# Gated experts and second MLP on one core: eight row slots, x of tiles 7 to 18 turned by VectorE, and loads issued by ScalarE

## Chip, cores and metric
One core of one Trainium2 chip runs the kernel. The metric is the device time of one execution in microseconds, the median of several runs. Engines: TensorE (PE), VectorE (DVE), ScalarE (ACT), GpSimd (POOL), SyncE (SP).

## What is computed
```python
# x: 2048 rows of 512; four experts, a token's id picks one
def experts(h, ids, W):                      # W[e]: 512 x 512, used three times
    e = min(clip(ids, 0, 24999) // 6250, 3)
    return (silu(h @ W[e].T) * (h @ W[e].T)) @ W[e].T
def mlp(h):                                  # 512 -> 1408 -> 512
    g = (h @ gate_w.T) * gate_s
    u = (h @ up_w.T) * up_s
    return (silu(g) * u) @ down_w.T * down_s
x = x + tanh(g_xattn) * experts(layernorm(x), ids, ctx)
x = x + tanh(g_ffn) * mlp(layernorm(x))
```
All three matrices of an expert are the same ctx_2048[e], so the kernel makes one product where gate and up have the same matrix. Each operand is split in a high part and the remainder, and a product runs in three passes (high x high, low x high, high x low).

## The kernel before, in words
**Routing.** A short part at the start sorts the tokens by expert into tiles of 128 rows of one expert each, at most 19 (`STEPS`), and makes the tables of row numbers `gidx` (gather) and `sidx` (store).

**Expert part.** Step k on PE: `first_product(k)` (12 matmuls; inner state z), `turn_x(k+1)` while x is turned by PE, `second_product(k-1)` (12 matmuls, waits `rows_ready` k, so for `update(k-2)`), and `turn_h(k)` (4 transposes of the hidden tile, waits `h_ready`). A tile goes this way: POOL gathers its rows into slot `ring_slot(k)` of `rows` (`gather`, L404), DVE makes its statistics (`stats`, L758), POOL the inverse deviation (`inverse_std`, L427), DVE the normalised tile (`norm`, L773, into `xn`), then x is turned (rows to columns), ACT writes the high part (`x_hi` or `turned_hi`), DVE the low part (`x_lo` or `turned_lo`). After the products DVE adds the result to the rows in the slot (`update`, L829), and POOL stores them to DRAM (`store`, L410). The slot is free when the store has landed: the gather of tile k+4 waits for store k-2, by one counter for all stores (L473).

**Two ways to turn x.** For tiles below `ON_PE` (11) PE turns it. From tile 11 on, SP's queue writes `xn` to DRAM and reads it back quarter by quarter (`turn_rows`, L336 to L345: first leg `turned_rows<-xn`, second leg `xq<-turned_rows`), and DVE transposes the 32x32 blocks of it (`turn`, L837, line L842). `norm(n+11)` waits until the first leg before it has landed; the second leg waits until the `turn` before it is done. Below it is called a bounce; bounce n is that of tile n + `ON_PE`.

**DVE's order in a step** is written out by hand: `step_on_pe(k)` (L851) is h_lo(k-1), norm(k+1), stats(k+2), hidden(k), x_lo(k+1), update(k-1); `step(k)` (L873), from k = 10 on, is h_lo(k-1), norm(k+2), turn(k+1-11), hidden(k), first half of the statistics of tile k+3, turned_lo(k+1), second half of them, update(k-1). hidden(k) (L820, "product" below) multiplies silu(z) by z and sets `h_ready`. `last_on_pe(9)` lies between. `first_stats(t)` (L787) makes the statistics of block row t of the second MLP's first block: 0 and 1 before step 9, 2 and 3 after steps 11 and 13.

**Loads.** Beside the bounces SP's queue holds, in written order, the MLP's weight rows (`weight_row`, L296, 704 KB each, eight), the down weights' check rows (`check_row`, L301, 256 KB each, eleven; each waits until ACT's `down_check` has freed its buffer) and the loads of the first block's rows (`load_half(0, 0)` and `(0, 1)`, L322, 528 KB each), which wait for the stores of their tokens. ACT in a step (L583): h_hi(k-1), weight_hi and weight_check of half a weight row, silu(k), x_hi or turned_hi of tile k+1, down_check.

**Second MLP.** Four blocks of four tiles, eleven chunks each: gate and up product (L1283), silu, product, down product (L1290). It starts when the last expert tile is in. Its first block's x comes from `first_norm`, `first_turn_x` (PE, L1147), `first_x_hi` and `first_x_lo` in steps 14 to 17, into the x buffer behind the expert weights in `work`, where `xq0`, `xt0` and `checked` lie before.

Of the kernel before, what the change touches and what calls it, by code (L numbers as in the profile page):

```python
# [39 lines left out]
RING = 6  # L40
ROWS = RING + BLOCK
# [6 lines left out]
PACKED = 15  # L48
EPS = 1e-5
# [5 lines left out]
ON_PE = 11  # L55
# [11 lines left out]
def ring_slot(k):  # L67

    return (k + 4) % RING


def row_slot(b, t):

    return t + RING * ((b + 1) % 2)
# [7 lines left out]
def build(nc, x, ids, ctxT, g_x, g_f, guT, dwT, gate_s, up_s, down_s, out):  # L82
# [7 lines left out]
    with ExitStack() as ctx:  # L90
# [12 lines left out]
        work = sb("work", [P, CTX_WORDS + XBUF_WORDS], F32R)  # L103
# [42 lines left out]
        xt0 = nc.alloc_sbuf_tensor_at("xt0", [P, D], F32, offset=work_base + (CTX_WORDS + 3 * D) * 4)  # L146
        wraw = nc.alloc_sbuf_tensor_at("wraw", [P, 2 * KC, 2, INTER], F32, offset=wgu_base)
# [65 lines left out]
        def token_of(first, last):  # L213

            return rows[:, first:last, D:D + 1].bitcast(U32)
# [30 lines left out]
        def quarter_rows(expert=False):  # L246

            return xq0[:, :] if expert else rows[:, RING - 2, 0:D]

        def turned_x(expert=False):  # L250

            return xt0[:, :] if expert else rows[:, RING - 1, 0:D]
# [4 lines left out]
        def down_w(c, s):  # L257
# [3 lines left out]
            row_landed w_hi w_lo down_hi down_lo  stored rows_a rows_b  # L261
# [9 lines left out]
        down_landed = [sem(f"down_landed{n}") for n in range(4)]  # L271
        last_stored = [sem(f"last_stored{t}") for t in range(BLOCK)]

        def hold(eng):

            eng.sem_inc(S["held"])

# [3 lines left out]
        def _(sp):  # L281
# [14 lines left out]
            def weight_row(r):  # L296
                if r:
                    sp.wait_ge(S["row_landed"], 16 * r)
                sp.dma_start(wraw[:, r, 1, :], gu_v[r // KC, r % KC]).then_inc(S["row_landed"], 16)

            def check_row(c):  # L301
                if c:
                    sp.wait_ge(S["check_landed"], 16 * c)
                if c >= 2:
                    sp.wait_ge(S["checks_done"], c)
                sp.dma_start(checked[:, c % 2, :], dw_v[c]).then_inc(S["check_landed"], 16)

            weight_row(0)
            check_row(0)
            check_row(1)  # L310
            weight_row(1)
            check_row(2)
            weight_row(2)
            check_row(3)
            sp.wait_ge(S["route_pe"], 4)
            sp.wait_ge(S["tables_ready"], 3)
            weight_row(3)
            check_row(4)
            weight_row(4)
            sp.wait_ge(S["ctx_lo"], len(ON_VECTOR))  # L320
            sp.wait_ge(S["pool_ctx_lo"], len(ON_POOL))
            def load_half(b, half_):  # L322
                t = BLOCK * b + 2 * half_
                at = row_slot(b, 2 * half_)
                if b == 0:
                    sp.wait_ge(S["stored"], 16 * (t + 2 + EXPERTS - 1))
                sp.dma_start(rows[:, at:at + 2, :], x1_v[:, t:t + 2, :])\
                  .then_inc((S["rows_a"], S["rows_b"])[half_], 16)

            for r in range(5, 2 * KC):  # L330
                check_row(r)
                weight_row(r)
            load_half(0, 0)
            check_row(8)

            def turn_rows(n):  # L336
# [3 lines left out]
                             xn[:, :].rearrange("p (i c) -> p i c", i=QUADS)).then_inc(S["xn_out"], 16)  # L340
# [6 lines left out]
            turn_rows(0)  # L347
            load_half(0, 1)
            check_row(9)
            turn_rows(1)  # L350
            check_row(10)
            for n in range(2, AHEAD):
                turn_rows(n)
            for c in range(IC):
                if c < 4:
                    sp.wait_ge(S["stored"], 16 * (TILES + c))
# [16 lines left out]
        def _(pool):  # L373
# [30 lines left out]
            def gather(k):  # L404
                at = ring_slot(k)
                pool.indirect_dma_start(  # L406
                    rows[:, at, 0:D], None, x, bass.IndirectOffsetOnAxis(ap=gidx[:, k:k + 1], axis=0))\
                    .then_inc(slot_landed[at], 16)

            def store(k):  # L410
                pool.indirect_dma_start(  # L411
                    scratch, bass.IndirectOffsetOnAxis(ap=sidx[:, k:k + 1], axis=0),
                    rows[:, ring_slot(k), :], None).then_inc(S["stored"], 16)
# [8 lines left out]
            def token_in(k, count=1):  # L422
                at = ring_slot(k)
                pool.tensor_copy(token_of(at, at + count), gidx[:, k:k + count].unsqueeze(2))\
# [7 lines left out]
            def first_inverse_std():  # L432
# [7 lines left out]
                rows[0:16, ring_slot(5), 0:D], None, x,  # L440
                bass.IndirectOffsetOnAxis(ap=inow[0:16, 0:1], axis=0)).then_inc(S["early_row"], 16)
            pool.memset(rows[:, 0:RING, D:WIDE], 0.0).then_inc(S["pads"], 1)
# [7 lines left out]
            pool.wait_ge(S["pads"], 1)  # L450
            token_in(0, 2)
            token_in(2, 4)
# [30 lines left out]
            for b in range(BLOCKS):  # L483
# [3 lines left out]
                for u in range(BLOCK):  # L487
# [6 lines left out]
                    else:  # L494
                        done = last_stored[t]
                    pool.indirect_dma_start(  # L496
                        out, bass.IndirectOffsetOnAxis(ap=token_of(row_slot(b, t), row_slot(b, t) + 1)[:, 0, :], axis=0),
# [3 lines left out]
        def _(act):  # L501
# [81 lines left out]
            def step(k, on_pe=False):  # L583
                h_hi(k - 1)
                weight_hi(k - PIECES_AT)
# [816 lines left out]
```

## Time and profile before
| | us |
|---|---|
| median of 3 runs | 386.21 |
| lowest, highest | 384.73, 387.35 |
| the profiled execution's own time | 384.71 |
| its span in the profile | 382.6 |
| PE busy | 364.2 (95% of the span) |
| DVE, ACT, POOL busy | 244.6, 147.5, 92.5 |

The span runs from the first to the last recorded instruction; 2.1 us of the execution's time lie around it. TensorE was granted its full clock nearly throughout. A step's bounds are taken at the start of `first_product` on PE; step 9 starts at 72.83 us, and the second MLP at 135.5 us.

### The profile page before, as it was taken

How to read it: one execution, taken by the hardware profiler on the slowest of the kernel's cores; microseconds unless marked ns; L12 is line 12 of the kernel's file. 1: busy time of each engine (PE TensorE's matmuls, PEld its weight loads, DVE VectorE, ACT ScalarE, POOL GpSimd, SP SyncE). 2: the span in 40 equal slices, each digit the busy share in tenths (PEclk: the TensorE clock that was granted, in tenths of full speed). 3: DMA queues.
4: the chain of work that ended last, by engine and by line, in shares of the span. 5: the costliest groups of instructions: out<-in, count | busy, mean ns of one | idle time of the engine just before them, and what ended most of it. 6: DMA issues, size and time to landing. Idle time of an engine off the chain costs nothing.

```text
span 382.6 us, 5569 instructions
## 1 busy us (share of the span) xinstructions
PE 364.2 (95%) x1704; PEld 298.0 (78%) x1704; DVE 244.6 (64%) x451; ACT 147.5 (39%) x266; POOL 92.5 (24%) x131
## 2 busy tenths in 40 slices
PE   3899999997999999999999999999999999999993
PEld 2478888786888878888888888888888888888892
DVE  6877666767998878779856256647346757323353
ACT  3466565646654536323322222322222322222230
POOL 7497454343461220011003110002201001300022
PEclk9999999999999999999999999999999999999998
DMA  6768876756654246432301412301232310200002
GB/s 224 274 217 259 260 275 195 261 142 222 218 165 142 84 140 192 140 86 57 82 0 55 169 55 83 82 0 55 76 119 69 95 27 27 82 0 0 0 29 86
DMA packets 27281, 45.39 MB, mean 119 GB/s; under 512 B 2928, under 2 KB 13168, under 8 KB 27264
## 3 DMA queue, kind: packets, MB, share of 16 engines
q1 hardware_dynamic: 22912, 30.83, 25.8%
q0 software_dynamic: 4352, 14.35, 10.4%
q8 instruction: 9, 0.15, 0.2%
q14 instruction: 8, 0.07, 0.1%
HBM read 30.59 MB, written 14.57 MB: 118 GB/s over the span
## 4 chain that ended last, share of the span: by engine, by line
PE 85%; DVE 6%; DMA 5%; issue 2%; POOL 1%; SPq 0%; ACT 0%; DVEq 0%; POOLq 0%
PE bank L1283 41%; PE bank L1178 21%; PE bank L1290 20%; DMA turned_rows<-xn 2%; PE bank L1193 2%; DMA rows<-x,gidx 2%; PE bank L1157 1%; DMA xq<-turned_rows 1%; PE bank L1147 0%; DVE rows L1060 0%; DMA ids_i<-ids 0%; DVE tmp L1053 0%; DVE parts L808 0%; DVE bn L763 0%; DVE xn L1053 0%
## 5 line engine op out<-in xcount | busy, mean ns | idle before, releaser
L1283 PE MATMUL bank<-work,wgu 128*128 (+1 forms) x736 | 167.3, 380 | 0.1
L1283 PEld LDWEIGHTS bank<-work,wgu 128*128 128x128 f32 x736 | 133.9, 188 | 27.1 <-issue 0.5
L1178 PE MATMUL bank<-work,parts 128*128 (+1 forms) x432 | 106.3, 397 | 2.0 <-ACT parts L522 1.7
L1178 PEld LDWEIGHTS bank<-work,parts 128*128 128x128 f32 x432 | 79.0, 188 | 18.8 <-issue 2.4
L1290 PE MATMUL bank<-work,hp 128*128 128x512 f32 x352 | 87.3, 390 | 0.2 <-DVE hp L1019 0.2
L1290 PEld LDWEIGHTS bank<-work,hp 128*128 128x128 f32 x352 | 65.7, 188 | 14.4 <-DVE hp L1019 0.6
L1000 DVE SCALAR_TENSOR_TENSOR sh<-bank,gs,sh 128x512 f32<-128x512 f32 x42 | 31.5, 749 | 55.4 <-PE bank L1283 55.4
L630 ACT ACTIVATE hp<-sh 128x512 fp32r<-128x512 f32 x42 | 26.6, 632 | 78.5 <-DVE sh L1000 78.5
L625 ACT ACTIVATE sh<-bank,gs 128x512 f32<-128x512 f32 x42 | 28.9, 688 | 72.0 <-PE bank L1283 71.2
L496 POOL DMA_INDIRECT out<-rows x16 | 16.2, 1011 | 128.3 <-DVE rows L1060 105.8
L1006 DVE TENSOR_TENSOR hp<-sh,hp 128x512 fp32r<-128x512 f32 x42 | 29.0, 691 | 22.3 <-ACT hp L630 22.3
L429 POOL TENSOR_TENSOR rstd<-ve,half 128x1 f32<-128x1 f32 x31 | 17.5, 564 | 104.4 <-DVE ve L770 104.2
L411 POOL DMA_INDIRECT x_rows<-rows,sidx x19 | 19.5, 1028 | 28.3 <-DVE rows L833 21.0
L406 POOL DMA_INDIRECT rows<-x,gidx x19 | 20.0, 1052 | 23.9 <-DMA x_rows<-rows,sidx 20.6
L763 DVE BATCH_NORM_STATS2 bn<-rows 128x6 f32<-128x512 f32 (+1 forms) x31 | 21.2, 684 | 0.8 <-DMA rows<-x,gidx 0.6
L531 ACT ACTIVATE parts<-bank 128x512 fp32r<-128x512 f32 x19 | 11.3, 596 | 25.0 <-PE bank L1193 22.5
L833 DVE SCALAR_TENSOR_TENSOR rows<-bank,tg,rows 128x512 f32<-128x512 f32 x19 | 14.2, 748 | 9.4 <-PE bank L1178 9.4
L822 DVE TENSOR_TENSOR sh<-bank,sh 128x512 f32<-128x512 f32 x19 | 13.1, 689 | 6.9 <-ACT sh L535 6.8
L535 ACT ACTIVATE sh<-bank 128x512 f32<-128x512 f32 x19 | 11.4, 598 | 12.5 <-PE bank L1178 11.1
L1043 DVE TENSOR_TENSOR work<-rows,work 128x512 f32 (+1 forms) x12 | 8.3, 692 | 9.7 <-ACT work L526 9.7
L826 DVE TENSOR_TENSOR parts<-bank,parts 128x512 fp32r<-128x512 f32 x19 | 13.0, 685 | 2.0 <-ACT parts L531 1.7
L842 DVE STREAM_TRANSPOSE rows<-rows 128x512 f32<-128x512 f32 x12 | 13.4, 1117 | 0.0
(134 smaller groups left out, 267.8 us busy)
## 6 DMA issues: line engine op xcount, KB each, us to landing
wraw<-guT SPq DMA_DIRECT2D x8, 704.0 KB
turned_rows<-xn SPq DMA_DIRECT2D x20, 256.0 KB
rows<-x_rows SPq DMA_DIRECT2D x8, 528.0 KB, 4.5
ctx_in<-ctxT SPq DMA_DIRECT2D x4, 1024.0 KB, 5.5
rows<-turned_rows SPq DMA_DIRECT2D x12, 256.0 KB
checked<-dwT SPq DMA_DIRECT2D x11, 256.0 KB
rows<-dwT SPq DMA_DIRECT2D x11, 256.0 KB, 2.8
xq<-turned_rows SPq DMA_DIRECT2D x8, 256.0 KB
```

The costliest lines, as they stand in the source:

```text
L406: pool.indirect_dma_start(rows[:, at, 0:D], None, x, bass.IndirectOffsetOnAxis(ap=gidx[:, k:k + 1], axis=0))\
L411: pool.indirect_dma_start(scratch, bass.IndirectOffsetOnAxis(ap=sidx[:, k:k + 1], axis=0), rows[:, ring_slot(k), :], None).then_inc(S["sto ...
L429: pool.tensor_tensor(rstd[:, 0:1], ve[:, 0:1], half[:, :], ALU.pow)\
L496: pool.indirect_dma_start(out, bass.IndirectOffsetOnAxis(ap=token_of(row_slot(b, t), row_slot(b, t) + 1)[:, 0, :], axis=0), rows[:, row_sl ...
L625: act.activation(sh[:, :], g_ps[:, :], ACT.Silu, scale=gs[:, 0, c:c + 1])\
L630: act.activation(hslot(c)[:, 0, :], sh[:, :], ACT.Copy).then_inc(S["hhi_ready"], 1)
L763: dve.bn_stats(bn[:, 0, :], rows[:, ds(at, 1), 0:D]).then_inc(S["bn_parts"], 1)
L1000: dve.scalar_tensor_tensor(out=sh[:, :], in0=u_ps[:, :], scalar=gs[:, 1, c:c + 1], in1=sh[:, :], op0=ALU.mult, op1=ALU.mult).then_inc(S["h ...
L1006: dve.tensor_tensor(hslot(c)[:, 1, :], sh[:, :], hslot(c)[:, 0, :].bitcast(F32), ALU.subtract).then_inc(S["hlo_ready"], 1)
L1178: mm = pe.matmul(out_ps[:, :], part(s)[:, c * P:(c + 1) * P], ctx_w(e, c, w), start=n == 0, stop=n == last)
L1283: mm = pe.matmul(out_ps[:, tiles.start * P:tiles.stop * P], wgu[:, row + h, w, c * P:(c + 1) * P], moving, start=n == 0, stop=n == last)
L1290: mm = pe.matmul(acc_ps[u][:, :], hslot(c)[:, s, u * P:(u + 1) * P], down_w(c, w), start=c == 0 and n == 0, stop=c == IC - 1 and n == len( ...
```

## The change
- `RING` goes from 6 to 8 row slots. Slots 6 and 7 (`far`) lie in the second MLP's x buffer in `work`; the MLP's own row slots stay where they were (`NEAR` = 6). Stores count on two semaphores, even and odd tiles (`tile_stored`). A gather is made for tile k+5 in POOL's iteration k and waits for store k-3.
- `ON_PE` goes from 11 to 7: x of tiles 7 to 18 is bounced and turned by DVE. The normalised tile for it has a buffer of its own (`xn_q`).
- DVE's `step(k)`, now from k = 6 on, makes turn, statistics of tile k+3, hidden, turned_lo, norm(k+3), then from k = 10 to 13 the statistics of block row k-10, and update last.
- Check rows 4 to 10 are issued by ACT in steps 5 to 11, weight rows 4 to 7 in steps 5, 7, 9 and 11 (`LOADS_AT`). ACT's loops over steps are written out. SP's queue holds the twelve bounces, `load_half(0, 0)` behind bounce 5 and `load_half(0, 1)` behind bounce 7.

```diff
-RING = 6
-ROWS = RING + BLOCK
+RING = 8
+NEAR = 6
+ROWS = NEAR + BLOCK
+LOADS_AT = {5: 4, 7: 5, 9: 6, 11: 7}
-ON_PE = 11
+ON_PE = 7
...
 def ring_slot(k):
-    return (k + 4) % RING
+    return (k + 2) % RING
...
+        xn_q = nc.alloc_sbuf_tensor_at("xn_q", [P, D], F32, offset=work_base + CTX_WORDS * 4)
+        far = nc.alloc_sbuf_tensor_at("far", [P, RING - NEAR, WIDE], F32,
+                                      offset=work_base + (CTX_WORDS + 6 * D) * 4)
+        def ring_rows(k, count=1):
+            at = ring_slot(k)
+            return rows[:, at:at + count, :] if at < NEAR else far[:, at - NEAR:at - NEAR + count, :]
+        def tile_stored(k):
+            return stored[k % 2], 16 * (k // 2 + 1)
+        def weight_row(eng, r):
+            if r:
+                eng.wait_ge(S["row_landed"], 16 * r)
+            eng.dma_start(wraw[:, r, 1, :], gu_v[r // KC, r % KC]).then_inc(S["row_landed"], 16)
+        def check_row(eng, c):
+            if c:
+                eng.wait_ge(S["check_landed"], 16 * c)
+            if c >= 2:
+                eng.wait_ge(S["checks_done"], c)
+            eng.dma_start(checked[:, c % 2, :], dw_v[c]).then_inc(S["check_landed"], 16)
@@ sync
-            weight_row(3)
-            check_row(4)
-            weight_row(4)
-            sp.wait_ge(S["ctx_lo"], len(ON_VECTOR))
-            sp.wait_ge(S["pool_ctx_lo"], len(ON_POOL))
+            weight_row(sp, 3)
-            for r in range(5, 2 * KC):
-                check_row(r)
-                weight_row(r)
-            load_half(0, 0)
-            check_row(8)
-            turn_rows(0)
-            load_half(0, 1)
-            check_row(9)
-            turn_rows(1)
-            check_row(10)
-            for n in range(2, AHEAD):
+            for n in range(AHEAD):
                 turn_rows(n)
+                if n in (5, 7):
+                    load_half(0, (n - 5) // 2)
@@ gpsimd
-            pool.memset(rows[:, 0:RING, D:WIDE], 0.0).then_inc(S["pads"], 1)
+            pool.memset(rows[:, 0:NEAR, D:WIDE], 0.0).then_inc(S["pads"], 1)
+            pool.memset(far[:, :, D:WIDE], 0.0).then_inc(S["pads"], 1)
...
             ctx_lo(5, 7)
+            gather(6)
+            token_in(6)
             for k in range(2, STEPS + 1):
-                if k < ON_PE:
+                if k <= ON_PE - 3:
                     inverse_std(k + 2)
+                if ON_PE - 3 <= k < STEPS - 3:
+                    inverse_std(k + 3)
                 if k == NORM_AT:
                     first_inverse_std()
-                pool.wait_ge(S["stored"], 16 * (k - 1))
-                if k + 4 < STEPS:
-                    gather(k + 4)
-                    token_in(k + 4)
-                if ON_PE - 1 <= k < STEPS - 3:
-                    inverse_std(k + 3)
+                if k > 2:
+                    pool.wait_ge(*tile_stored(k - 3))
+                if k + 5 < STEPS:
+                    gather(k + 5)
+                    token_in(k + 5)
@@ scalar
-            def step(k, on_pe=False):
+            def step(k):
                 h_hi(k - 1)
+                if k > 4 and k < IC + 1:
+                    check_row(act, k - 1)
+                if k in LOADS_AT:
+                    if LOADS_AT[k] == 5:
+                        act.wait_ge(S["ctx_lo"], len(ON_VECTOR))
+                        act.wait_ge(S["pool_ctx_lo"], len(ON_POOL))
+                    weight_row(act, LOADS_AT[k])
                 weight_hi(k - PIECES_AT)
                 weight_check(k - PIECES_AT)
                 silu(k)
...
             step(16)
+            act.wait_ge(*tile_stored(13))
             first_x_hi(1)
@@ vector
             def step_on_pe(k):
                 h_lo(k - 1)
-                norm(k + 1, ring_slot(k + 1))
+                norm(k + 1)
                 landed(k + 2)
-                stats(k + 2, ring_slot(k + 2))
+                stats(k + 2, ring_rows(k + 2)[:, :, 0:D])
                 hidden(k)
                 x_lo(k + 1)
+                if k == ON_PE - 3:
+                    norm(k + 2)
+                    landed(k + 3)
+                    stats(k + 3, ring_rows(k + 3)[:, :, 0:D])
                 update(k - 1)
             def last_on_pe(k):
                 h_lo(k - 1)
-                norm(k + 1, ring_slot(k + 1))
-                landed(k + 2)
-                stats(k + 2, ring_slot(k + 2))
+                norm(k + 2)
+                landed(k + 3)
+                stats(k + 3, ring_rows(k + 3)[:, :, 0:D])
                 hidden(k)
                 x_lo(k + 1)
-                norm(k + 2, ring_slot(k + 2))
+                norm(k + 3)
                 update(k - 1)
-                landed(k + 3)
-                stats(k + 3, ring_slot(k + 3))
-            def step(k):
+            def step(k, block_row=None):
                 h_lo(k - 1)
-                if k + 2 < STEPS:
-                    norm(k + 2, ring_slot(k + 2))
-                if k + 1 > ON_PE:
-                    turn(k + 1 - ON_PE, True)
-                hidden(k)
-                if k + 1 == ON_PE:
-                    turn(0, True)
+                turn(k + 1 - ON_PE, True)
                 if k + 3 < STEPS:
                     landed(k + 3)
-                    begin_stats(ring_slot(k + 3))
+                    stats(k + 3, ring_rows(k + 3)[:, :, 0:D])
+                hidden(k)
                 turned_lo(k + 1)
                 if k + 3 < STEPS:
-                    end_stats(k + 3)
+                    norm(k + 3)
+                if block_row is not None:
+                    first_stats(block_row)
                 update(k - 1)
...
             for k in range(EXPERTS, ON_PE - 2):
                 step_on_pe(k)
-            first_stats(0)
-            first_stats(1)
             last_on_pe(ON_PE - 2)
-            for k in range(ON_PE - 1, NORM_AT):
-                step(k)
-                if k % 2:
-                    first_stats((k - STATS_AT) // 2 + 2)
+            for k in range(ON_PE - 1, 14):
+                step(k, k - STATS_AT if k >= STATS_AT else None)
             step(14)
```

## Rows read from the trace of the kernel before
**Rows 1.** The page: shares of the chain that ended last, by engine
```profile
PE 85%; DVE 6%; DMA 5%; issue 2%; POOL 1%; SPq 0%; ACT 0%; DVEq 0%; POOLq 0%
```
**Rows 2.** Busy time in the steps of the expert part; columns as named
```profile
core 0: us, PE busy (x) PEld busy (x) DVE busy (x) ACT busy (x) POOL busy (x), PEclk, DMA share, GB/s
...
47.21:53.61 6.40, 6.40 (x33) 5.28 (x33) 4.12 (x9) 3.78 (x8) 3.92 (x6) 1.00 0.64 228
...
72.83:79.94 7.11, 6.41 (x33) 5.03 (x32) 6.02 (x16) 3.89 (x8) 3.89 (x6) 1.00 0.27 92
79.94:87.77 7.83, 6.18 (x31) 4.91 (x30) 5.36 (x10) 3.84 (x8) 2.82 (x4) 1.00 0.83 241
87.77:94.53 6.76, 6.41 (x29) 4.87 (x29) 4.84 (x10) 4.18 (x11) 1.87 (x3) 1.00 0.69 232
94.53:100.67 6.14, 6.14 (x29) 5.17 (x30) 6.00 (x15) 3.76 (x8) 3.82 (x6) 1.00 0.54 172
100.67:106.58 5.91, 5.91 (x29) 4.90 (x29) 5.35 (x11) 3.28 (x6) 2.65 (x4) 1.00 0.66 204
```
**Rows 3.** The chain that ended last: start us, length us, what
```profile
60.02 2.77 PE bank L1178 x12
62.79 0.44 PE bank L1157 x4
...
74.19 0.61 DVE bn L790
...
79.04 3.82 DMA turned_rows<-xn
...
84.26 4.88 DMA turned_rows<-xn
89.16 2.74 DMA xq<-turned_rows
```
**Rows 4.** SyncE's queue: start us, length us, queue, line, issue
```profile
82.89 0.33 SPq L344 DMA_DIRECT2D xq<-turned_rows  x1
83.26 0.45 SPq L327 DMA_DIRECT2D rows<-x_rows  x1
...
97.81 0.37 SPq L339 DMA_DIRECT2D turned_rows<-xn  x1
100.27 0.32 SPq L344 DMA_DIRECT2D xq<-turned_rows  x1
```
**Rows 5.** VectorE in step 5, in order of time
```profile
47.88 0.69 DVE L826 TENSOR_TENSOR parts<-bank,parts 128x512 fp32r<-128x512 f32 x1 [0.32 <-issue]
```
**Rows 6.** VectorE in step 14, in order of time
```profile
106.18 0.75 DVE L833 SCALAR_TENSOR_TENSOR rows<-bank,tg,rows 128x512 f32<-128x512 f32 x1
106.85 0.68 DVE L790 BATCH_NORM_STATS2 bn<-rows 128x6 f32<-128x512 f32 x1
...
107.86 0.68 DVE L826 TENSOR_TENSOR parts<-bank,parts 128x512 fp32r<-128x512 f32 x1
108.45 0.60 DVE L784 TENSOR_SCALAR xn<-rows,mv,rstd 128x512 f32<-128x512 f32 x1
108.98 1.08 DVE L842 STREAM_TRANSPOSE xt<-xq 128x512 f32<-128x512 f32 x1
110.02 0.69 DVE L822 TENSOR_TENSOR sh<-bank,sh 128x512 f32<-128x512 f32 x1
...
112.11 0.75 DVE L833 SCALAR_TENSOR_TENSOR rows<-bank,tg,rows 128x512 f32<-128x512 f32 x1
```
**Rows 7.** ScalarE in step 7, in order of time
```profile
61.95 0.19 ACT L552 ACTIVATION_READ_ACCUMULATOR junk<-wraw  x1
62.83 0.60 ACT L535 ACTIVATE sh<-bank 128x512 f32<-128x512 f32 x1 [0.69 <-PE bank L1178]
```
**Rows 8.** Landing of block-row loads (L327): all eight, then that of 65.4 us
```profile
DMA to landing us min/median/max: 3.6/4.5/6.3
...
DMA to landing us min/median/max: 6.3/6.3/6.3
```

More of the change, by code:

```diff
@@ L211, in token_half, with ring_row, token_of @@
             return slice(i * D // 2, (i + 1) * D // 2)
-        def token_of(first, last):
-            return rows[:, first:last, D:D + 1].bitcast(U32)
+        def ring_rows(k, count=1):
+            at = ring_slot(k)
+            return rows[:, at:at + count, :] if at < NEAR else far[:, at - NEAR:at - NEAR + count, :]
+        def ring_row(k):
+            return ring_rows(k)[:, 0, 0:D]
+        def token_of(b, t):
+            return rows[:, row_slot(b, t), D:D + 1].bitcast(U32)
         def first_xt(i):
@@ L591, in step @@
                     turned_hi(k + 1)
-            with act.Fori(PIECES_AT, ON_PE - 1) as k:
-                step(k, on_pe=True)
-                down_check(k - PIECES_AT)
-            with act.Fori(ON_PE - 1, IC + PIECES_AT) as k:
+            for k in range(PIECES_AT, 15):
                 step(k)
-                down_check(k - PIECES_AT)
-            for k in range(IC + PIECES_AT, 15):
-                step(k)
+                if k - PIECES_AT < IC:
+                    down_check(k - PIECES_AT)
             step(15)
@@ L756, in store_table, with stats, begin_stats @@
                    .then_inc(S["tables_ready"], 1)
-            def stats(m, at):
-                begin_stats(at)
+            def stats(m, row):
+                begin_stats(row)
                 end_stats(m)
-            def begin_stats(at):
-                dve.bn_stats(bn[:, 0, :], rows[:, ds(at, 1), 0:D]).then_inc(S["bn_parts"], 1)
+            def begin_stats(row):
+                dve.bn_stats(bn[:, 0, :], row).then_inc(S["bn_parts"], 1)
             def end_stats(m):
@@ L894, in first_x_halves @@
                     part = slice(i * HALF, (i + 1) * HALF)
-                    dve.tensor_scalar(xn[:, part], rows[:, ring_slot(0), part], mv[:, 0, 0:1], rstd[:, 0:1],
+                    dve.tensor_scalar(xn[:, part], ring_row(0)[:, part], mv[:, 0, 0:1], rstd[:, 0:1],
                                       ALU.subtract, ALU.mult).then_inc(S[ready], 1)
@@ L906, in _ @@
             landed(0)
-            stats(0, ring_slot(0))
+            stats(0, ring_rows(0)[:, :, 0:D])
             store_table()
@@ L929, in _ @@
             ctx_lo(6, 7)
-            norm(3, ring_slot(3))
+            norm(3)
             h_lo(1)
@@ L934, in _ @@
             landed(4)
-            stats(4, ring_slot(4))
+            stats(4, ring_rows(4)[:, :, 0:D])
             update(1)
-            norm(4, ring_slot(4))
+            norm(4)
             ctx_lo(7, 9)
@@ L942, in _ @@
             landed(5)
-            stats(5, ring_slot(5))
+            stats(5, ring_rows(5)[:, :, 0:D])
             update(2)
@@ L1026, in next_stats @@
                     dve.wait_ge((S["rows_a"], S["rows_b"])[t // 2], 16 * (b + 1))
-                stats(STEPS + BLOCK * (b - 1) + t, row_slot(b, t))
+                stats(STEPS + BLOCK * (b - 1) + t, rows[:, ds(row_slot(b, t), 1), 0:D])
             def next_norm(b, t):
```

90 lines of the change are left out of this document (40 added, 50 removed).

## The prediction
> **What bounds the kernel now.** I read the page first: TensorE (PE) holds 85% of the chain of work that ended last, so what can be won lies in PE work that is removed and in the stretches where PE stands [rows 1]. From the start of the second MLP (135.5 us) on, the chain is matmul after matmul, and what moves that start moves the end by as much. Then I cut the expert part at the starts of its steps: a step with both turnings on PE takes 6.40 us, one with only the hidden tile's turning 5.91 us [rows 2]. The difference between the first two, 0.49 us, is one turning of x (0.44 us in the chain, [rows 3]) with what surrounds it. Against these lengths step 9 is 0.71 us too long (7.11 - 6.40), step 10 1.92 (7.83 - 5.91), step 11 0.85 (6.76 - 5.91), step 12 0.23 (6.14 - 5.91) [rows 2]: 3.71 us in all. The chain names their causes: in step 9 two statistics of block rows stand on DVE ahead of what PE waits for, and in steps 10 and 11 x of tiles 11 and 12 is late from its bounce through DRAM, whose first legs take 3.82 and 4.88 us and a second leg 2.74 us [rows 3].
>
> **What the change takes away.** (a) x of tiles 7 to 10 is no longer turned by PE: four steps (6 to 9) go from 6.40 to 5.91 us: 4 x 0.49 = 1.96 us. (b) The start of the bounces moves from the loaded steps 9 to 11 to step 5, and the norm is made for tile k+3 at the end of step k, where it was made for tile k+2 near the step's beginning. With the order of [rows 6] the norm comes 3.6 us later in a step but one whole step of 5.91 us earlier for its tile, 2.3 us more lead. If all of it is covered, the 3.71 us go. Most that can be won: 1.96 + 3.71 = 5.67 us.
>
> **Are the bounces in time?** The first leg took 2.46 us in a quiet step (issued 97.81, the second leg issued on its landing at 100.27, [rows 4]) and 3.82 to 4.88 us in loaded ones [rows 3]. A new norm waits for the first leg before it, so bounces can follow each other every 0.54 + 0.1 + 4.88 = 5.5 us, below 5.91. The first one: norm(7) comes in step 5 (start 47.21, [rows 2]) after h_lo, which began at 47.88 there [rows 5] and has the next instruction 0.59 later [rows 6]: about 48.5 to 49.0; out lands 52.9 to 53.9, second leg 55.7 to 56.7; transpose 1.09, stats 1.01, product 0.65 [rows 6] end at 58.5 to 59.5. PE turns the hidden tile of step 6 at 53.61 + 5.47 = 59.08 (5.91 less the turning's 0.44). So 0 to 0.4 us are lost once; I take 0.2. Steps 6 to 9 move more than before: a bounce adds two times 256 KB to a step that moved 228 GB/s at a DMA share of 0.64 [rows 2]. Against that, weight rows (704 KB) now come every second step.
>
> **ACT as issuer.** Check rows in steps 5 to 11 and weight rows in steps 5, 7, 9 and 11 are issued by ACT behind h_hi. The trace has no issue on ACT; on SP one takes 0.32 to 0.45 us [rows 4], so I bound it by 0 and 0.8 us for two. In a step, ACT's check ends at 62.14 and silu starts at 62.83, when PE is done [rows 7]: 0.69 us are free. What is over, 0.1 us, meets the product's own slack: silu begins 2.81 us into its step (60.02, [rows 3]), with its 0.60 and the product's 0.65 that is 4.06, and PE turns at 5.47: 1.4 us. Queued behind the issuing instructions are only those two weight passes and silu. Cost 0; without this cover at most 0.8 us in each of four steps. The ACT loop written out, the wait of first_x_hi(1) for store 13 (made two steps before) and the second memset cost nothing that PE sees: the memset lies ahead of gather(0), which waits for its index. POOL's wait of a gather for the store two steps before goes with eight slots, but PE never waited for POOL there. gather(6) ahead of inverse_std(4) makes rstd of tile 4 up to 1.3 us later, while its norm has over 2 us until PE's turning: 0. DVE gets four more transposes in place of none on PE; a step such as 5 held 4.12 us of DVE work [rows 2], with 1.09 more it stays below 5.91.
>
> **What comes back.** Here I count against the change. Statistics of block row 0 now stand in DVE's step 10, ahead of update(9), and their rows are loaded behind bounce 5 in SP's queue. Let T be the start of step 10 on PE.
> - Bounce 5's second leg needs turn(4), which DVE makes in step 10 at T+1.3 to T+2.35 (h_lo starts 0.67 into the step, as in [rows 5], lasts 0.59, then 1.04 for the transpose, [rows 6]). Second leg at T+2.4, load_half(0,0) 0.37 us behind it as in [rows 4], T+2.75. Such a load landed in 3.6 to 6.3 us, median 4.5 [rows 8]: T+7.25.
> - DVE comes to these statistics at T+5.2 (product at 4.06, then 0.59 for x_lo and 0.53 for the norm), waits 2.1 us, ends them (1.01, [rows 6]) at 8.3 and update(9) at 9.0. PE's second product of tile 10 wants it at T + 5.91 + 2.77 = 8.68: 0.35 us. DVE then does h_lo 0.59, turn 1.04, stats 1.01, product 0.65 and is at 12.3; PE wants the product at 9.03 + 2.75 = 11.8: 0.5 us more. Step 12 starts at 12.75 where 11.82 was due: 0.9 late.
> - Block row 2 in step 12 waits in the same way for load_half(0,1) behind bounce 7, whose second leg needs turn(6). DVE, at its limit with statistics in each of steps 10 to 13 (112.11 - 106.18 = 5.93 us of unbroken work with one in it, [rows 6], and 0.12 more since the parts no longer interlock), makes turn(6) at 16.65; load at 17.1, landed (4.1, a little quieter) at 21.2. Statistics and update end at 22.95; PE wanted them at 18.8 + 2.76 = 21.56: 1.4 us. The product behind them costs 0.6 again, and the rest of steps 12 to 14 0.3.
> Sum 0.9 + 1.4 + 0.6 + 0.3 = 3.2, say 3.3 us. With a landing of 3.6 us for both it is 1.8; with 6.3 for both 7.2. I take 4.5 and 4.1 because the loads stand among a gather, a store and a check row, as the one issued at 83.26 did.
>
> A rule of the Trainium skill bears on the moved issues ("DMA: Bandwidth & Descriptors", Issuing engines are not separate DMA queues): transfers started from any engine share the same 16 DMA engines and interleave, and another issuer saves only the sequencer's time. The first leg that stood behind a 528 KB load and a check row on one queue took 4.88 us [rows 3, 4]; by the rule it is no quicker beside a 704 KB row on ACT's queue. By the sum this changes nothing while 5.5 stays below 5.91, but it speaks for the third rival below.
>
> **The sum.** -1.96 - 3.71 + 0.2 + 3.3 = -2.2 us. The profiled execution had 384.71 us (span 382.6 and 2.1 around it), 1.5 below the median of 386.21. So 382.5 for an execution like it, and 384.0 as the median. A change of 1% (3.9 us) is about what a measurement of this kernel can tell from none.
>
> **Rivals.**
> - Full gain, 380.5 (386.2 - 5.7), up to 382.4 with the quick landing: load_half lands in 3.6 us or the late updates are absorbed. For it: the lower end of [rows 8], and PE's wants lie only 0.35 us before the first update. Against it: DVE has no slack in four steps running. Chance 0.27.
> - Loads land late, 387.9: both take the 6.3 us that the one of step 7 took beside a weight row [rows 8]: -5.67 + 0.2 + 7.2 = +1.7. Against it: weight row 6 is issued a step before the first. Chance 0.15.
> - Bounces starve, slower than before: in steps 7 to 11 the first leg shares the DMA engines with weight, check, gather and store. It decides from a first leg of 5.3 us on (5.91 less 0.6). At the 6.3 us of [rows 8] bounces come every 6.95 us, 1.04 too slow in five steps, +5.2. With the late loads: 386.2 - 5.67 + 5.2 + 7.2 = 393; alone 389. Against it: nothing above 4.88 was seen in a first leg. Chance 0.10.
> - The forecast, two waits of DVE for block rows that give back over half: 0.48.
>
> **Numbers.** Likeliest 384.0, its own range 382.5 to 385.5. Over all: 380.4 to 387.6. Faster by over 1% (below 382.35): 0.27 of the first rival and a little of the forecast's edge, 0.30. Slower by over 1% (above 390.1): 0.07 from the third rival. The rest, 0.63, lies within 1%.
>
> **What would show it.** PE steps of 5.91 us from step 6 to 9, with no idle time over 0.5 us at the first bounce; in steps 10 and 12 DVE idle by 1.5 to 2.5 us ahead of the block rows' statistics, released by the load of rows, and PE waiting 0.3 to 2 us for update and then product; second-MLP start at 133.3 instead of 135.5. If that start is at 130, the waits were covered; if first legs last over 5.3 us in steps 7 to 11, the third rival holds; if silu comes over 1 us after PE's first product, ACT's issues cost what I put at nothing.

## The result, and the profile after

The changed kernel takes 397.0 us (median of 4, 395.25 to 399.51), the kernel before 385.94 (median of 4 with the run beside it): a ratio of 1.029, 95% interval 1.022 to 1.036. Forecast were 384.0 and a gain. The profiled execution of the changed kernel has 396.57 us with a span of 394.5, 11.9 more than the 382.6 of before.

Where do they lie? The second MLP starts at 141.81 us where it started at 135.53, so 6.3 us are lost ahead of it, and it lasts 252.7 us to the end of the span where it lasted 247.1: 5.6 us are lost in a part that the change doesn't touch.

First the expert part. The chain of the changed kernel, in order of time (start, length, what), from the first bounce on:

```profile
49.59 5.57 DMA turned_rows<-xn_q
...
55.17 3.38 DMA xq<-turned_rows
...
58.58 1.09 DVE xt L857
```

The same view for the next bounces:

```profile
62.34 6.13 DMA turned_rows<-xn_q
68.48 4.88 DMA xq<-turned_rows
...
77.15 6.83 DMA turned_rows<-xn_q
...
88.72 3.65 DMA rows<-x_rows
...
92.39 0.71 DVE bn L806
```

These first legs last 5.57, 6.13 and 6.83 us, where 4.88 was the longest before [rows 3]; two second legs take 3.38 and 4.88 us for 2.74. The three are the legs issued within 1.5 us of weight rows 4, 5 and 6 (steps 5, 7 and 9); the one beside row 7 landed after 4.8 us. The first legs of the steps between them landed 3.5, 5.0 and 3.6 us after their issue. At 88.72 comes the load of block rows and behind it the statistics of block row 0. What PE waited for, in order of time (what stands in brackets is the idle time ahead of an instruction and what ended it; the lines of its idle stretches alone):

```profile
61.31 0.66 PE L1203 MATMUL bank<-ident,sh 128*128 128x128 f32 x4 [1.45 <-DVE sh L838]
...
76.13 0.66 PE L1203 MATMUL bank<-ident,sh 128*128 128x128 f32 x4 [2.05 <-DVE sh L838]
77.00 7.40 PE L1188 MATMUL bank<-work,parts 128*128 x24 [0.22 <-issue]
...
94.49 3.06 PE L1188 MATMUL bank<-work,parts 128*128 x12 [0.69 <-DVE rows L849]
...
108.45 3.06 PE L1188 MATMUL bank<-work,parts 128*128 x12 [1.07 <-DVE rows L849]
```

The waits at 61.31 and 76.13, 1.45 and 2.05 us, are for the product on DVE (`hidden`, "sh L838"), which stands behind the transposition of a late bounce. The two for "rows L849", 0.69 and 1.07 us, are the updates behind the block rows' statistics. A wait costs more than its own length: from one `first_product` to the next the steps with the first two take 8.34 and 8.75 us, those with the other two 7.58 and 7.93, and a step without a wait 6.02. And the 24 matmuls that start at 77.00, right behind the wait of 2.05 us, take 7.40 us, where 24 take 5.83 in the steps around. The windows of these steps show why, answering to [rows 2] (busy time of the engines, then granted clock, DMA share and GB/s):

```profile
core 0: us, PE busy (x) PEld busy (x) DVE busy (x) ACT busy (x) POOL busy (x), PEclk, DMA share, GB/s
60.10:68.30 8.20, 6.75 (x33) 5.42 (x33) 6.41 (x14) 4.73 (x11) 4.81 (x7) 1.00 0.75 243
68.30:77.00 8.70, 6.43 (x30) 4.79 (x29) 5.24 (x10) 4.13 (x9) 2.28 (x3) 1.00 0.70 187
77.00:84.68 7.68, 7.68 (x29) 6.16 (x30) 5.11 (x11) 3.71 (x8) 3.56 (x6) 0.78 0.83 265
84.68:90.70 6.02, 6.02 (x30) 4.83 (x28) 4.69 (x9) 3.94 (x8) 2.22 (x3) 1.00 0.72 239
```

In the step from 77.00 on the mean granted clock is 0.78 of 2.4 GHz: for 44% of the time PE had the lower level of 1.2 GHz. At the full clock the stretch takes 1.6 us less. Before, every step from 28 us on to the second MLP had 1.00 ([rows 2] show six of them).

SyncE's and ScalarE's queues around the first bounce, the counterpart to [rows 4 and 7]:

```profile
47.75 0.40 ACTq L307 DMA_DIRECT2D checked<-dwT  x1
48.18 0.44 ACTq L300 DMA_DIRECT2D wraw<-guT  x1
48.75 0.79 ACT L553 ACTIVATE wgu<-wraw 128x704 fp32r<-128x704 f32 x1 [0.47 <-issue]
...
50.13 0.19 ACT L564 ACTIVATION_READ_ACCUMULATOR junk<-wraw 128x1 f32 x1
50.48 0.60 ACT L547 ACTIVATE sh<-bank 128x512 f32<-128x512 f32 x1 [0.16 <-PE bank L1188]
```

ACT issues a check row and a weight row in 0.84 us, and silu still starts when PE is done (0.16 us of idle time ahead of it, ended by PE). So it is in each of the steps 5 to 11: 0.16 to 2.25 us of idle time ahead of silu, always ended by PE. The weight row is under way when the first leg is issued at 49.59.

Now the second MLP. The chain there, before and after, between 300 and 340 us of each span, first before:

```profile
302.92 3.63 PE bank L1283 x16
306.54 1.81 PE bank L1290 x8
```

and after:

```profile
302.10 3.71 PE bank L1293 x16
305.82 1.86 PE bank L1300 x8
```

Sixteen products of gate and up take 3.71 us for 3.63, eight of down 1.86 for 1.81, without idle time and at a granted clock of 1.00 in both. That is 2.2 to 2.8% on the products of the MLP. The expert part has it too, but less: 12 products take 2.80 us there for 2.77 [rows 3], 1.1%, and a step without stalls 6.02 for 5.91, 1.9%.

### The profile page after: what moved, and what is told of

It is laid out like the page before. It is cut to its first block, busy times and chain, and to the rows that moved or that the text cites. A ratio compares the mean times of both kernels' runs of the same rounds, so it can differ in the third digit from the quotient of the medians.

```text
span 394.5 us, 5406 instructions
## 1 busy us (share of the span) xinstructions
PE 372.9 (95%) x1688; PEld 298.3 (76%) x1688; DVE 247.4 (63%) x455; ACT 148.0 (38%) x266; POOL 94.1 (24%) x132
## 4 chain that ended last, share of the span: by engine, by line
PE 77%; DMA 12%; DVE 7%; issue 2%; POOL 1%; ACT 0%; SPq 0%; DVEq 0%; POOLq 0%
PE bank L1293 42%; PE bank L1300 20%; PE bank L1188 13%; DMA turned_rows<-xn_q 6%; DMA xq<-turned_rows 2%; DMA rows<-x_rows 2%; DMA rows<-x,gidx 2%; PE bank L1203 1%; DVE xt L857 1%; DMA x_rows<-rows,sidx 1%; DVE xn_q L800 1%; DVE bn L779 1%; DVE rows L849 1%; DVE sh L838 1%; PE bank L1157 0%
## 5 line engine op out<-in xcount | busy, mean ns | idle before, releaser
L1293 PE MATMUL bank<-work,wgu 128*128 (+1 forms) x736 | 171.1, 385 | 0.0
L1188 PE MATMUL bank<-work,parts 128*128 (+1 forms) x432 | 109.2, 405 | 2.8 <-DVE rows L849 1.8
L1188 PEld LDWEIGHTS bank<-work,parts 128*128 128x128 f32 x432 | 80.5, 191 | 23.1 <-issue 5.3
L1300 PE MATMUL bank<-work,hp 128*128 128x512 f32 x352 | 88.9, 394 | 0.2 <-DVE hp L1029 0.2
L419 POOL DMA_INDIRECT x_rows<-rows,sidx x15 | 15.4, 1027 | 35.4 <-DVE rows L849 34.3
L779 DVE BATCH_NORM_STATS2 bn<-rows 128x6 f32<-128x512 f32 (+1 forms) x27 | 18.1, 670 | 0.7 <-DMA rows<-x,gidx 0.7
L838 DVE TENSOR_TENSOR sh<-bank,sh 128x512 f32<-128x512 f32 x19 | 13.1, 687 | 7.6 <-ACT sh L547 7.6
L414 POOL DMA_INDIRECT rows<-x,gidx x15 | 16.3, 1085 | 4.3 <-issue 2.4
L857 DVE STREAM_TRANSPOSE xt<-xq 128x512 f32<-128x512 f32 x12 | 13.1, 1093 | 5.5 <-DMA xq<-turned_rows 5.5
L1203 PE MATMUL bank<-ident,sh 128*128 128x128 f32 x72 | 11.1, 277 | 4.4 <-DVE sh L838 4.4
L1203 PEld LDWEIGHTS bank<-ident,sh 128*128 128x128 f32 x72 | 8.5, 141 | 7.5 <-DVE sh L838 6.1
```

The costliest lines, as they stand in the source:

```text
L779: dve.bn_stats(bn[:, 0, :], row).then_inc(S["bn_parts"], 1)
L838: dve.tensor_tensor(sh[:, :], z_ps[:, :], sh[:, :], ALU.mult).then_inc(S["h_ready"], 1)
L857: dve.transpose(turned_x(expert).rearrange("p (h a g) -> p g h a", h=KC, g=QUADS), quarter_rows(expert).rearrange(order, g=QUADS, h=KC))\
L1188: mm = pe.matmul(out_ps[:, :], part(s)[:, c * P:(c + 1) * P], ctx_w(e, c, w), start=n == 0, stop=n == last)
L1203: mm = pe.transpose(ht_ps[:, c * P:(c + 1) * P], sh[:, c * P:(c + 1) * P], ident[:, :])
L1293: mm = pe.matmul(out_ps[:, tiles.start * P:tiles.stop * P], wgu[:, row + h, w, c * P:(c + 1) * P], moving, start=n == 0, stop=n == last)
```

## The experiments

Two things had to be explained, and I began with a theory for each. Theory S: `work` became 32 words longer (`2 * (WIDE - D)`; e2 takes this line back), to hold the far slots with their pads, and all tensors behind it, `wgu` and `parts` among them, now lie 128 bytes further. Theory C: the bounces' first legs starve beside the loads, above all beside the weight rows.

### Shift and contention
**e1**, the kernel before with the shift alone:
```diff
-        work = sb("work", [P, CTX_WORDS + XBUF_WORDS], F32R)
+        work = sb("work", [P, CTX_WORDS + XBUF_WORDS + 32], F32R)
```


> The kernel before with 32 unused words behind work, so that everything allocated after it lies 128 bytes further, as in the changed kernel; nothing else differs. In the changed kernel the second MLP lasts 252.7 us where it lasted 247.1, without idle time. If the shift makes every product slower (theory S), this kernel loses 5.6 us in the MLP and about 1 us in the expert part: 392.5, and a step there takes 6.46 where it took 6.40. If the slow products come from something else in the change or from the chip (rival), it stays at 386 with steps of 6.40.

Measured: 393.08 us against 386.11, ratio 1.016 (1.007 to 1.025). Its products in the MLP (chain, as above):

```profile
303.40 3.73 PE bank L1283 x16
307.13 1.86 PE bank L1290 x8
```

3.73 and 1.86 us, as in the changed kernel. 32 unused words cost 7 us. In the profiled execution the MLP lasts 252.8 us as forecast, 5.7 more than before, and starts at 137.59 us, 2.1 later; 1.15 of these are a longer wait of PE in step 11 (2.81 us for 1.66).

**e2**, the changed kernel without the shift:
```diff
-        work = sb("work", [P, CTX_WORDS + XBUF_WORDS + 2 * (WIDE - D)], F32R)
+        work = sb("work", [P, CTX_WORDS + XBUF_WORDS], F32R)
...
-        far = ... offset=work_base + (CTX_WORDS + 6 * D) * 4)
+        far = ... offset=work_base + (CTX_WORDS + XBUF_WORDS - 2 * WIDE) * 4)
...
             step(15)
+            act.wait_ge(*tile_stored(12))
             first_x_hi(0)
```
`checked`, `xq0` and `xt0` lie one tile lower to make room.

> The changed kernel with its two far slots placed so that work keeps its old length (the buffers behind xn_q lie one tile lower, one more wait for a store made two steps before). Theory S: the MLP goes back to 247.1 us and good steps from 6.03 to 5.91, about 390.5 in all, the 6 us lost in the bounces stay. Rival: 397, MLP at 252.7.

Measured: 391.9 us, ratio to before 1.014 (1.004 to 1.024). Its products are back:

```profile
302.70 3.63 PE bank L1294 x16
306.32 1.81 PE bank L1301 x8
```

Theory S holds from both sides: 7 us added to one kernel, 5 taken from the other. Of what e2 has over before, 5.8 us, 5.15 are the expert part's: its MLP starts at 140.68 us, where it started at 135.53.

**e3**, check rows cut, and **e4**, weight rows later, both on the changed kernel:
```diff
+            cols = slice(0, D if c < 4 else 32)
-            eng.dma_start(checked[:, c % 2, :], dw_v[c])
+            eng.dma_start(checked[:, c % 2, cols], dw_v[c][:, cols])
```


> The changed kernel with check rows 4 to 10 reduced to their first 32 columns (the rest of their check is left out), so 240 KB less move in each of steps 5 to 11. If the first legs are slow because of what moves beside them (theory C), those of 5.57, 6.13 and 6.83 us fall to about 4.5 and 2 to 3 us of PE's idle time in steps 6 to 9 go: 394. If they are slow of themselves (a new source buffer, an early start), they and the time stay: 397.

Measured: 395.65 us (2 runs), 1.3 less than the changed kernel, whose own runs lie 4 us apart: the times alone don't tell the two apart. First legs by SP's queue, from the issue of the first leg to that of the second (which can hold a wait for the `turn` before it): 4.51, 4.02, 6.37, 4.05, 6.05 us, where the changed kernel has 5.58, 3.90, 6.14, 5.41 and 6.85. Those beside weight rows 5 and 6 stay over 6 us; the first, beside weight row 4, and the fourth fall by over 1 us. PE's two waits for the product fall from 1.45 and 2.05 us to 0.67 and 0.90, but a third of 0.49 us comes, and the waits for update grow from 1.8 to 3.4 us. Right in direction, and less than half the time expected.

```diff
-LOADS_AT = {5: 4, 7: 5, 9: 6, 11: 7}
+LOADS_AT = {8: 4, 10: 5, 12: 6, 14: 7}
```


> The changed kernel with weight rows 4 to 7 issued in steps 8, 10, 12 and 14 instead of 5, 7, 9 and 11. Theory C (the 704 KB rows on the other queue take the bounces' share): first legs in steps 5 to 7 fall below 5 us, idle time there goes (some 3.5 us), while the legs in steps 8 and 10 grow: 394 to 396. Rival (legs slow of themselves, or for gathers and stores): first legs in steps 5 and 7 stay at 5.6 to 6.2 us, 397.

Measured: 401.4 us (2 runs), 4.4 slower than the changed kernel instead of 1 to 3 faster. The first legs did what theory C says: those of steps 5 to 7 fell to 3.25, 4.55 and 4.73 us. What I had not seen is where the rows went. Weight row 5 (issued at 81.04, landed 6.1 us later) now moved beside bounce 5, whose first leg took 6.5 us, so that the first load of block rows behind it left 7.1 us into step 10, where it left 4.1 us into it before this edit. In SP's queue (start, length, issue):

```profile
87.77 0.45 SPq L344 DMA_DIRECT2D rows<-x_rows  x1
88.28 0.48 SPq L350 DMA_DIRECT2D turned_rows<-xn_q  x1
98.25 0.33 SPq L356 DMA_DIRECT2D xq<-turned_rows  x1
```

The first of the lines is the load of block rows. It was issued within 0.7 us of a check row, a second leg and the first leg of bounce 6, and landed 7.0 us after its issue, where it took 3.6 in the changed kernel; the first leg landed after 7.3 us. (The 9.97 us from its issue to that of the second leg are more than the leg, for the second leg waits for `turn` of the bounce before, which DVE made late.) DVE stood 6.82 us for the block rows (until 94.80), and PE 7.1 us for the update behind their statistics (its next 12 products took 4.77 us, where 3.05 is usual):

```profile
PE bank L1188 <- DVE rows L849: 9.4, 2, 7.1
```

Weight row 6 (issued at 102.16, landed 6.3 us later) moved beside the second load of block rows, which took 6.1 us for 4.1 and made the second wait, 2.3 us. So what moves beside a transfer decides how long it takes, and the miss shows that the block rows' loads suffer by it as the first legs do.

### What else stands in the way
The next four rest on e2.

**e5**, block rows two bounces earlier:
```diff
-                if n in (5, 7):
-                    load_half(0, (n - 5) // 2)
+                if n in (3, 5):
+                    load_half(0, (n - 3) // 2)
```


> The changed kernel without the shift (as in e2) and with the two loads of block rows behind bounces 3 and 5 instead of 5 and 7, two steps ahead of the statistics that want them. In e2 PE stands 2.4 and 0.3 us for update behind these waits and its clock falls in the first. If the waits for block rows cost what I worked out (theory B, 3.3 us), it gains 3 to 4 us on e2: 388. If the loads only crowd the bounces of steps 8 and 10 (rival), PE's idle time moves there and it stays at 391 to 392.

Measured: 389.79 us (median of 10), ratio to before 1.006 (1.002 to 1.010) where e2 had 1.014. Half of the expected 3 to 4 us at most: 2.1 us between the medians, and the two intervals overlap. PE no longer waits for the first of the updates, but the legs issued 2.2 and 1.8 us behind the loads of block rows, each beside a weight row as well, take 7.5 and 8.6 us in the trace (of an execution of 391.83 us, the longest of the ten). e6 and e7 have such a leg without a weight row beside it.

**e6**, eight bounces as before, but eight slots and the loads on ACT:
```diff
-ON_PE = 7
+ON_PE = 11
-LOADS_AT = {5: 4, 7: 5, 9: 6, 11: 7}
+LOADS_AT = {5: 4, 6: 5, 7: 6, 8: 7}
...
+            load_half(0, 0)
             for n in range(AHEAD):
                 turn_rows(n)
-                if n in (5, 7):
-                    load_half(0, (n - 5) // 2)
+                if n == 0:
+                    load_half(0, 1)
```


> e2 with x turned by PE up to tile 10 as before (eight bounces), weight rows 4 to 7 issued by ACT in steps 5 to 8, load_half(0,0) ahead of bounce 0 and (0,1) behind it: eight slots and the loads on ACT without the early bounces. If the early bounces beside the weight rows are what costs (theory C), no first leg exceeds 5 us, PE's stalls of before (3.7 us) mostly go, and it beats before: 383 to 384. If the issues on ACT, the eight slots or the new order on DVE cost by themselves (rival), it stays above 386.

Measured: 385.75 us against 386.14, ratio 0.998 (0.995 to 1.001): no difference that can be told, where 383 to 384 was expected. The slots, the new order and the issues on ACT cost nothing that can be told, but there are stalls as before, for another reason:

```profile
82.45 0.38 SPq L344 DMA_DIRECT2D rows<-x_rows  x1
82.87 0.47 SPq L350 DMA_DIRECT2D turned_rows<-xn_q  x1
89.91 0.33 SPq L356 DMA_DIRECT2D xq<-turned_rows  x1
```

Bounce 1 stands 0.42 us behind load_half(0, 1) and takes 7.04 us; PE waits 0.78 and 1.37 us in the steps that follow. (This trace is of an execution of 388.59 us, the longest of the ten. It also has a wait of 2.06 us ahead of 21.75 us, before all bounces, where the traces of before and after have 0.87; e7 and e11 have 2.05 and 2.04 there.)

**e7**, ten bounces (`ON_PE = 9`, weight rows as in e6, block rows behind bounces 1 and 3):

> As e6 with bounces from tile 9 on (ten) and the block rows' loads behind bounces 1 and 3. Theory C: bounces 0 and 1 stand beside weight rows 6 and 7 and one of their first legs is over 5 us; 384 to 386, between e6 and e5. Rival (the number of bounces doesn't matter): like e6, less 1 us for two turnings saved.

Measured: 388.72 us, ratio 1.006 (1.002 to 1.009), 3 us slower than e6 and slower than expected. The first legs of bounces 1 and 2 take 6.64 and 7.10 us, the former 0.7 us behind the issue of weight row 7, the latter 0.4 us behind the block rows' load. So a bounce counts by what moves beside it; that PE turned two tiles less won nothing here.

**e8**, weight rows in halves:
```diff
-                if k in LOADS_AT:
+                if 5 <= k < 13:
...
-                    weight_row(act, LOADS_AT[k])
+                    weight_half(act, k + 3)
```
with `row_landed` counted by halves.

> e5 with the weight rows loaded in halves, one of 352 KB in each of steps 5 to 12 in place of 704 KB in every second. Theory C with a limit by the burst: the longest first legs (6 us in the steps with a row) fall below 5.3 us and the time to 385 to 386. If what counts is the whole amount that moves in these steps (rival), all first legs are about 5 us and the time stays with e5.

Measured: 392.93 us, ratio 1.018 (1.013 to 1.024), slower than e5. This run doesn't tell the two cases apart, for it brought a wait of its own: the halves wait for each other, so the last ones of rows 0 to 3 are issued late on SP, and ACT, in whose order `weight_half` stands ahead of silu, stood for one of them:

```profile
47.54 0.48 ACTq L312 DMA_DIRECT2D checked<-dwT  x1
54.46 0.33 ACTq L301 DMA_DIRECT2D wraw<-guT  x1
54.92 0.79 ACT L558 ACTIVATE wgu<-wraw 128x704 fp32r<-128x704 f32 x1 [6.84 <-DMA wraw<-guT]
```

6.84 us of idle time ahead of 54.92, PE stood 4.34 us for the product behind it, and its next 24 products took 8.07 us. This is a cost of ACT as an issuer that I had not reckoned: not the issue, but what the issue waits for. In the changed kernel it doesn't arise. The first legs of bounces 1 to 3, beside one half each, landed after 3.6, 2.4 and 3.7 us; this speaks for the burst, but is not shown by a time.

### The way out, and the alignment
**e9**, e6 with both loads of block rows ahead of bounce 0:
```diff
             load_half(0, 0)
+            load_half(0, 1)
             for n in range(AHEAD):
                 turn_rows(n)
-                if n == 0:
-                    load_half(0, 1)
```


> e6 with load_half(0,1), too, ahead of bounce 0 in SP's queue. In e6 the first leg of bounce 1 stood behind this 528 KB load and took 7.04 us, and PE stood 0.8 and 1.4 us and more around it. If a leg is slow for what is ahead of it in its queue and beside it (theory C), no first leg exceeds 5 us here, 3 to 4 us of stalls go, and it beats before: 382 to 383. Rival (the stalls of steps 10 and 11 come from DVE's order): 385.5 as e6.

Measured: 384.37 us (median of 12) against 385.84, ratio 0.995 (0.992 to 0.998): 0.5% faster than the kernel before, less than expected. The first legs are 4.19, 5.33, 3.97 us from issue to issue, the second of them 4.9 us to its landing. In the profiled execution, of 385.85 us and so 1.5 above the median, one stall is left, and it shows the clock again. PE's timeline:

```profile
87.22 0.65 PE L1204 MATMUL bank<-ident,sh 128*128 128x128 f32 x4 [1.85 <-DVE sh L839]
88.10 7.36 PE L1189 MATMUL bank<-work,parts 128*128 x24 [0.23 <-issue]
```

and the windows of this step and the one behind it:

```profile
88.10:95.60 7.50, 7.50 (x27) 6.01 (x28) 6.38 (x14) 3.64 (x8) 3.80 (x6) 0.77 0.58 182
95.60:101.60 6.00, 6.00 (x32) 4.99 (x30) 5.75 (x13) 3.78 (x8) 2.97 (x4) 1.00 0.54 170
```

A wait of 1.85 us, then 24 matmuls in 7.36 us for 5.75: the clock adds 1.6 us to it, nearly as much again. Whether the shorter executions have it too no trace shows.

**e10**, the kernel before shifted by 256 bytes (`+ 64` in place of e1's `+ 32`), and **e11**, by 128 bytes behind `wgu`:
```diff
+        gap_words = sb("gap_words", [P, 32], F32)
         parts_base = nc.sbuf_base
```


> The kernel before with 64 unused words behind work: a shift of 256 bytes in place of e1's 128. If odd multiples of 128 bytes are what slows the products (an alignment of 256 bytes), it stays at 386, with 3.63 us for 16 products. If any shift does it, or the relation to a larger power of two, about 393 and 3.71 us.

Measured for e10: 385.49 us, ratio 1.000 (0.996 to 1.004). Its products: 3.63 and 1.81 us.

```profile
301.54 1.81 PE bank L1290 x8
303.35 3.63 PE bank L1283 x16
```

> The kernel before with 32 unused words behind wgu: parts (x and hidden of the experts, two of the three h buffers of the MLP), and all after it lie 128 bytes further, work and wgu stay. If a product slows by the address of its own stationary tile, the gate and up products keep 3.63 us for 16, while the expert steps (6.46 for 6.40) and the down products (1.86 for 1.81 us for 8) are slow: 388 to 389. If something shared (rows, tables, code) does it, all are slow: 393. If wgu's address alone does it, nothing is slow: 386.

Measured for e11: 390.12 us (388.76 and 391.48), ratio 1.010 (1.003 to 1.017). The profiled execution is the longer one, with the early wait of 2.04 us told at e6 and products at the lower clock behind it. The chain:

```profile
203.01 1.81 PE bank L1291 x8
...
301.79 1.86 PE bank L1291 x8
303.65 3.63 PE bank L1284 x16
```

Gate and up products (stationary tile in `wgu`, which has not moved) keep 3.63 us; down products (stationary tile in `parts`) take 1.86; expert products, stationary tile in `parts` as well, take 2.80 us for 12. The line at 203.01 tells most: the down product of a block's last chunk, once in eleven, has its stationary tile in the third h buffer, which lies in `work` and has not moved, and it keeps 1.81 us; in e1 and the changed kernel it keeps 1.82. The moving operand lies in `work`, unmoved, in all of these. So the product slows by the place of its own stationary tile: 128 bytes from the old place cost, 256 don't. Other distances were not tried.

**e12**, e5 with almost nothing beside the bounces:
```diff
-LOADS_AT = {5: 4, 7: 5, 9: 6, 11: 7}
+LOADS_AT = {5: 4, 14: 5, 15: 6, 16: 7}
```
and the reduced check rows of e3; ACT's passes over rows 5 to 7 work on rows 0 to 2, so the kernel leaves out the high parts of rows 5 to 7.

> e5 (no shift, block rows early, twelve bounces) with almost nothing beside the bounces: weight rows 5 to 7 are loaded in steps 14 to 16, where the bounces have an end (ACT meanwhile converts and checks rows 0 to 2 again in their place, so the high parts of rows 5 to 7 are left out), and check rows 4 to 10 are reduced to 32 columns. Only gathers, stores, weight row 4 and the two loads of block rows move beside the bounces. Theory C (bounces starve by the loads beside them): first legs after the first stay under 5 us, PE's stalls go, and the 5.7 us that I had put as the most that can be won come: 380.5 to 382. Rival (bounces from tile 7 on are too slow for a step of 5.91 us by themselves, or DVE is, with twelve transposes): stalls of 3 us and more stay, 385 to 388.

Measured: 381.92 us (median of 7) against 385.55, ratio 0.992 (0.989 to 0.995). One wait of PE is left in the steps with bounces, for the product behind the first of them:

```profile
60.36 0.66 PE L1206 MATMUL bank<-ident,sh 128*128 128x128 f32 x4 [0.76 <-DVE sh L840]
```

and the MLP's start, in the chain:

```profile
131.92 7.75 PE bank L1296 x32
```

The same twelve bounces, the same DVE order, and the MLP starts at 131.9 us, 3.6 ahead of before and 8.8 ahead of e2. First legs of the first six bounces: 4.73, 3.70, 3.82, 3.66, 3.74, 3.50 us. Theory C holds, and a gain of 3.6 us is there when the loads are elsewhere. Bounces 4 and 6 follow the loads of block rows by 1.8 and 2.0 us here and take 3.74 and 3.62 us: such a load alone, at that distance, does not slow the leg behind it. Behind it by 0.4 us the leg was slow (e6, e7), and by 1.3 us with a weight row beside it as well (e2: 7.3 us).

## Why the prediction was wrong, point by point

**What can be won, 5.67 us: right as a bound.** Steps of 5.91 to 5.94 us exist from step 7 on where nothing is late (e12). There 3.6 of the 5.67 us came; step 6 took 7.36 us, 1.45 too long, for the one wait that is left.

**"Are the bounces in time?": the step that failed.** I bounded the first leg by 4.88 us, the longest seen, and so had bounces every 5.5 us, below a step. The first legs beside weight rows took 5.57, 6.13 and 6.83 us, two second legs 3.38 and 4.88 us where I had reckoned 2.8, and the first six bounces followed each other every 6.3 to 8.0 us. 4.88 came from steps in which no weight row moved, and I had carried it to steps with one, where the only row that I had of a transfer beside a weight row said 6.3 us [rows 8]. I named the DMA share of a loaded step, 0.64, and added 512 KB to it without reckoning what it leaves. This was my third rival, "bounces starve", and its chance (0.10) was far too low; its sign, first legs over 5.3 us, came in steps 7 and 9. PE lost its time where DVE makes the product behind a late transposition: steps 6 and 8 are 2.3 and 2.7 us longer than 6.02, for which I had 0.2 in all. Even e12, whose first leg of 4.73 us is within my bound, lost 1.45 us at the first bounce, so the 0.2 was too small by itself: the product was done at 60.3 us, where I had 58.5 to 59.5. The rule of the Trainium skill that I weighed ("DMA: Bandwidth & Descriptors", Issuing engines are not separate DMA queues), that transfers from all engines share the same 16 DMA engines, agrees with these traces: with the rows on ACT's queue the legs on SP's took up to 6.83 us, and in e4 (5.57 to 3.25 us) and e9 (7.04 to 4.9) first legs fell when the bytes themselves moved elsewhere.

**"What comes back": right in mechanism, and in size.** DVE waited 1.51 us at 92.39 and 2.03 at 106.35 for block rows, each where I had put it and in the 1.5 to 2.5 us that I had named, and PE 0.69 and 1.07 us for the updates behind. The two steps of PE are 1.56 and 1.91 us longer than 6.02, 3.5 us for my 3.3. In part the terms offset each other: the first load left 4.1 us into step 10, not 2.75, for `turn(4)` was late, and landed in 3.65 us, not 4.5. What I left out is what such a load does to the bounce that follows at once: 7.04 and 7.10 us for its first leg in e6 and e7, where the legs before and behind it in e6 took 3.3 and 4.0 us.

**ACT as issuer, cost 0: right for the changed kernel** (0.84 us of issues, silu on time). It does not carry over to an issue that has to wait: in e8 that cost ACT 6.84 us ahead of silu.

**A term missing altogether: the second MLP.** I took it as given that what moves its start moves its end by as much. The 32 words at the end of `work` were part of the change, and I passed over them. They cost 5.6 us in the MLP and 1 to 1.5 in the expert part (an estimate from e1 and from the 0.1 us by which the steps without stalls are longer).

**A second one: the clock.** I priced idle time of PE at its length. In the changed kernel the longest wait (2.05 us) was followed by a stretch at 1.2 GHz that costs 1.6 more; in e2 it happened twice, for 3 us.

In sum for the profiled executions: forecast -2.2, measured +11.9; of the 14.1 between them 5.6 are the MLP's shift and 8.5 the expert part's (its end at 141.8 us for a forecast 133.3). Of these 1 to 1.5 are the shift there, 1.6 the clock, 4.9 steps 6 and 8 with their late bounces (beyond my 0.2), and the rest, under 1, I can't assign.

## What to carry to other kernels

Before work is moved to a time when it needs transfers, add up what the DMA engines carry in that stretch, and take a transfer's price from a row with the same neighbours, not from the longest among lighter ones; that the neighbour is issued by another engine did not help here. Where an edit changes a tensor's length, see what stands behind it: here 128 bytes on the stationary tiles cost more than the whole edit could win, and a shift of 256 bytes costs nothing (e10). Price a wait of PE with the clock that it may lose behind it.

## What the runs showed of the hardware that was not expected

- A shift by 128 bytes of the tensor that holds the stationary tiles slows the MLP's fp32r products with 512 moving columns from 3.63 to 3.71 or 3.73 us for 16 (2.2 to 2.8%), those of the expert part from 2.77 to 2.80 for 12; 256 bytes change nothing (e10). Which unit makes the difference is not shown.
- After waits of 1.85 (e9) and 2.05 us (the changed kernel), but not after 1.45 us there, PE's next 24 products took 7.36 and 7.40 us for 5.75 and 5.83, at a mean granted clock of 0.77 and 0.78. Length alone does not decide: in e2 a wait of 1.58 us was followed by 24 products in 7.36 us, while e1's wait of 2.81 us was followed by 24 in 5.84 us, the usual time of a shifted kernel. What does was not tried.
- A first leg of 256 KB landed 2.3 us after its issue in a quiet step of the changed kernel (issued at 118.31), 3.9 (e2) to 6.8 us (changed kernel) beside a weight row, and 7.0 to 7.5 us where a block rows' load stood ahead of it (e6, e7, and e4 and e8 with more beside it).
